# Audio tower on one core: the fused loop over 32 pairs of sequences in another order, relative scores added by TensorE

## What is computed

```python
# t: token mixer
h = depthwise_conv(x, 7 taps) + b_dw; h = relu(w_pw @ h + b_pw); h = max over pairs of rows   # 125 -> 62 rows
y = real(fft2(h)); y = normalised over 192 * gamma + beta
# a: attention with relative positions, 8 heads of 64, values of 96
q = (x @ Wq) * 64**-0.5
scores = (q + r_w_bias) @ k^T + relative_shift((q + r_r_bias) @ r_k^T)
y = softmax(scores) @ v @ Wo + bo
# f: feed-forward with 8-bit activations and ternary weights
xq = clip(round(rmsnorm(x) * 127 / max|.|), -128, 127) / scale
gate, up = split(xq @ w_in^T); y = quantised(rmsnorm(silu(gate) * up)) @ w_out^T
# b: rotary attention, 12 heads of 16 with 3 key heads
# r: router picks one of 8 experts for each row; then the experts, each a gated layer of 512
```

## Time and profile before

| | us |
|---|---|
| median of 3 runs | 1287.79 (1283.11 to 1289.89) |
| the profiled execution | 1298.94 |
| its span, first to last instruction | 1297.1 |
| PE busy | 1066.9 |
| DVE busy | 928.2 |
| ACT busy | 728.9 |
| POOL busy | 350.3 |

### The profile page before, as it was taken

How to read it: one execution, slowest core, us unless ns; L and a number is a source line. 1 busy time by engine, 2 the same in 40 slices (tenths; PEclk the granted TensorE clock), 3 DMA queues, 4 the chain that set the end, 5 groups by cost and what they waited for, 6 DMA issues and landing times.

```text
span 1297.1 us, 30154 instructions
## 1 busy us (share of the span) xinstructions
PE 1066.9 (82%) x9054; PEld 818.0 (63%) x9055; DVE 928.2 (72%) x2959; ACT 728.9 (56%) x2417; POOL 350.3 (27%) x968
## 2 busy tenths in 40 slices
PE   2658998888888888888888888888898652899995
PEld 1536666666666666666666666666666431788884
DVE  2347888888887888888888888888887542355553
ACT  2425766666666666666666666666666430333331
POOL 2012233323322222233332323323322112122222
PEclk9888999999999999999999999999999665899999
DMA  6053011111111111111111111111111004322211
GB/s 202 31 163 91 31 43 35 35 35 37 49 38 42 40 35 35 35 35 35 35 35 35 35 41 35 35 35 36 50 40 35 7 7 157 89 56 58 55 54 40
DMA packets 48910, 65.65 MB, mean 51 GB/s; under 512 B 6573, under 2 KB 39120, under 8 KB 48752
## 3 DMA queue, kind: packets, MB, share of 16 engines
q1 hardware_dynamic: 38656, 46.47, 11.4%
q0 software_dynamic: 4512, 12.52, 2.9%
q10 hardware_dynamic: 5712, 6.29, 1.7%
HBM read 36.61 MB, written 28.95 MB: 51 GB/s over the span
## 4 chain that ended last, share of the span: by engine, by line
issue 49%; DVE 18%; POOL 14%; PE 9%; ACT 5%; DMA 2%; POOLq 1%; SPq 1%; DVEq 0%; ACTq 0%
PE bank_a L566 3%; PE bank_b L566 2%; DVE conv_hi L1137 2%; DVE f_gate L1229 2%; DVE amax_y L1230 1%; POOL rstd_f L513 1%; DVE o L1211 1%; DVE conv_lo L1133 1%; PE bank_t L566 1%; POOL rstd_a L513 1%; POOL rstd_t L486 1%; POOL rstd_b L513 1%; POOL rstd_y L497 1%; POOL hold_a L526 1%; DVE res_b L1271 1%
## 5 line engine op out<-in xcount | busy, mean ns | idle before, releaser
L1133 DVE SCALAR_TENSOR_TENSOR conv_lo<-xT_lo,c_taps,conv_lo 128x248 f32<-128x248 f32 x192 | 90.2, 470 | 25.9 <-ACT conv_hi L900 16.3
L491 POOL TENSOR_TENSOR var_y<-ssq_y,c_eps 128x1 f32<-128x1 f32 x32 | 6.1, 190 | 357.2 <-ACT f_sq L1000 357.2
L978 ACT ACTIVATE b_in<-res_b,norm_shift_f,rstd_f 128x192 f32<-128x192 f32 x32 | 17.5, 546 | 120.0 <-POOL norm_shift_f L516 120.0
L1029 ACT ACTIVATE p<-bank_b,max 128x62 f32<-128x62 f32 x384 | 80.6, 337 | 6.1 <-DVE max L1308 6.1
L566 PE MATMUL bank_a<-e_xT,w_now 128*128 128x128 f32 x544 | 70.5, 284 | 12.1 <-DVE e_gate L1420 9.0
L1299 DVE TENSOR_TENSOR kBD_lo<-bank_b,c_blocks 128x1024 f32<-128x1024 f32 x32 | 39.2, 1224 | 56.3 <-PE bank_b L569 56.3
L566 PE MATMUL bank_a<-c_wv,a_xT 64*64 64x384 f32 (+1 forms) x512 | 78.7, 500 | 0.1
L566 PEld LDWEIGHTS bank_a<-e_xT,w_now 128*128 128x128 f32 x544 | 64.9, 196 | 21.4 <-DVE w_now L1416 11.0
L1415 DVE COPY w_now<-w_sb 128x512 f32 x34 | 14.5, 427 | 86.8 <-PE bank_a L566 78.4
L566 PE MATMUL bank_a<-c_wo,oT 128*128 128x192 f32 x384 | 74.9, 347 | 1.9 <-ACT oT L866 1.9
L566 PE MATMUL bank_a<-a_xT,c_wq 64*128 64x128 f32 (+1 forms) x512 | 74.8, 288 | 1.6 <-ACT a_xT L866 1.6
(11 more groups left out here) (259 smaller groups left out, 3138.9 us busy)
## 6 DMA issues: line engine op xcount, KB each, us to landing
rel_scores<-rel_tok SPq DMA_DIRECT2D x32, 492.0 KB, 2.6
rel_skew<-rel_scores SPq DMA_DIRECT2D x64, 124.0 KB, 2.8
x_tok<-in_x SPq DMA_DIRECT2D x32, 187.5 KB
e_rest<-routed SPq DMA_DIRECT2D x34, 97.0 KB
e_tok<-routed SPq DMA_DIRECT2D x34, 96.0 KB, 1.9
routed<-pad_rows SPq DMA_DIRECT2D x8, 386.0 KB, 2.9
w_sb<-in_w ACTq DMA_DIRECT2D x1, 3072.0 KB, 12.2
...
```

Of the source, the lines that this page charges most:

```text
L978: nc.scalar.activation(dst, src, ACT.Identity, scale=rstd[k][:, :], bias=shift[k][:, :]).then_inc(done, 1)
L1029: last = nc.scalar.activation(p1[:, h, 0:T], src[:, at * T:(at + 1) * T], ACT.Exp, bias=max1[:, h:h + 1])
L1133: c.mark(v.scalar_tensor_tensor(conv_lo[:, :, :], xT_lo[:, :, k:k + PAIRS], c_taps[:, 0, k:k + 1], conv_lo[:, :, :], ALU.mult, ALU.add))
```

## The change

The stages get another order on all engines, and other lags: the whole of part b but its residual now lies in one turn (lag 4), the end of f (`f_transpose_y`, `f_down`) goes from lag 4 to lag 3, the end of a (`a_transpose_heads`) from 3 to 2, its beginning (`a_transpose`) from 2 to 1. POOL's lags are one higher than before, since its list begins at another stage. Beside the order, these stages do other work:

- **Relative scores.** `a_scores` leaves its accumulation open, and a new stage `a_add_relative` on PE multiplies the identity with `rel_skew` (128 rows, 496 columns) onto the same bank. DVE takes only the maxima, from the bank, and ACT the exponentials, from the bank. `s` and L1197 are gone. `rel_tok` and `rel_skew` have the head ahead of the position, so the copy back from DRAM is made of runs of 62 numbers (248 bytes) where it had runs of 248 numbers (992 bytes).
- **The bias of q.** DVE computes `qr` only; ACT makes `qw` from it with four additions of the difference of the biases (`a_bias_qw`).
- **Quantising.** DVE stops at the scale (`scale_of`). ACT rounds in two steps (`f_round_x`, `f_round_y`), POOL multiplies out the `dequant` factors. The clip at 127 falls away.
- **Key blocks.** `kBD_lo` has four blocks instead of eight; `b_scores` multiplies 64 rows at a time, six products of 248 columns where there were two of 496 and two of 248.
- **Token mixer.** The last 64 channels of the two sequences lie at partitions 0 and 64, so that `t_pointwise` has products of 124 columns for each half, `t_pool` and `t_relu` half the elements in their second instruction, and `t_dft` one product on 128 rows and two of 64.

```diff
+            def a_add_relative(m):
+                pe.wait_ge(a_rel, 32 * m + 32)
+                mm(pa1[:, 0:H0 * T].rearrange("p (h a s) -> p h a s", h=HP, a=2), ident[:, :],
+                   rel_skew[:, :, :, :].rearrange("p a h s -> p h a s"), start=False).then_inc(a_s, 1)
...
             def a_max_scores(m):
-                dve.wait_ge(a_s, 2 * m + 2)
-                dve.wait_ge(a_rel, 32 * m + 32)
-                c.link(v.tensor_tensor(s0..., pa1..., rel_skew..., ALU.add))
-                v.tensor_reduce(max0[:, :], s0[:, :, :], axis=AX.X, op=ALU.max, negate=True).then_inc(a_shift, 1)
+                dve.wait_ge(a_s, m + 1)
+                v.tensor_reduce(max0[:, :], pa1[:, 0:H0 * T]..., op=ALU.max, negate=True).then_inc(a_shift, 1)
...
-                    last = nc.scalar.activation(p0[:, h, 0:T], s0[:, h, :], ACT.Exp, bias=max0[:, h:h + 1])
+                    last = nc.scalar.activation(p0[:, h, 0:T], pa1[:, h * T:(h + 1) * T], ACT.Exp, bias=max0[:, h:h + 1])
...
+            def a_bias_qw(m):
+                act.wait_ge(a_qrr, m + 1)
+                after_previous(act, a_s, m)
+                for hp in range(HP):
+                    last = nc.scalar.activation(qw[:, hp, :], qr[:, hp, :], ACT.Identity, bias=bias_step[:, hp:hp + 1])
+                last.then_inc(a_qwr, 1)
...
+                def stage(m):     # f_round
+                    act.wait_ge(qsc_ready[k], m + 1)
+                    nc.scalar.activation(work, work, ACT.Identity, scale=qsc[k][:, 0:1], bias=magic[:, 0:1]).then_inc(rounded_of[k], 1)
+                    act.wait_ge(rounded_of[k], m + 1)
...
+                    nc.scalar.activation(dst, work, ACT.Identity, bias=magic[:, 1:2]).then_inc(done, 1)
...
-                        rel_skew[TP * b:TP * b + TP, :, :, :].rearrange("p a s h -> p a (s h)"),
-                        bass.AP(rel_dram.tensor, b * TP * 2 * RW + (T - 1) * HP,
-                                [[2 * RW - HP, TP], [RW, 2], [1, T * HP]])).then_inc(a_rel, 16)
+                        rel_skew[TP * b:TP * b + TP, :, :, :].rearrange("p a h s -> p (a h) s"),
+                        bass.AP(rel_dram.tensor, b * TP * 2 * RW + T - 1,
+                                [[2 * RW - 1, TP], [REL, 2 * HP], [1, T]])).then_inc(a_rel, 16)
...
             overlapped(pe, (
...
+                (1, t_transpose), (3, a_output), (2, a_project), (4, b_transpose), (4, b_project), (2, a_relative),
+                (1, t_pointwise), (4, b_transpose_qk), (2, a_project_v), (3, f_transpose_x), (4, b_scores),
```

280 lines of the change are left out of this document (149 added, 131 removed).

## The result

| | before | after |
|---|---|---|
| median, us (measured together) | 1288.39 (1283.11 to 1289.89) | 1219.70 (1216.75 to 1221.79) |
| the profiled execution | 1298.94 | 1219.23 |
| its span | 1297.1 | 1217.4 |

The ratio is 0.9462, 95% interval 0.9433 to 0.9491: 68.7 us less. The forecast was 1220.

A forecast was written before the change was run, and what follows sets the result against it. No engine was full: a circle of waits through DVE and PE, plus PE's half clock, set the 30.7 us turn. PE's 25.6 plus waits gave 28.7; 28 turns save 56 us, ends 12: 1220 us, range 1168 to 1274.

The forecast's parts named there:

- The circle and the clock: Old turn: DVE's list is in the circle of waits some 19 us, PE's some 10; half clock costs 1.7 us.
- Rival B: The low clock stays or ACT's rounding is dearer: turn 29.4 to 30.4, 1243 to 1271 us; chance 0.18.
- Work taken from DVE between those points shortens the turn at once: Between the transposed keys from PE and DVE's residual, where DVE works almost without a gap; no separate size given.
- a walk through the new lists: New stage lists followed once round until PE's start came back: turn 28.55 us, taken as 28.7.
- DVE and ACT: Busy time per turn: DVE 4.0 us less, to 21.7; ACT 3.6 more, less 0.3, to 23.8.
- PE at full clock: PE's work per turn: 27.25 - 1.7 + 0.84 - 0.4 - 0.4 = 25.6 us, making it the fullest engine.
- The waits of PE: Six waits in PE's new list, together 2.95 us a turn on top of its work.
- The copy back: `rel_skew` through DRAM lands 6.0 to 7.9 us after `rel_tok`; PE's product comes at 8.5, so the wait is hidden.
- rival E: Short runs cost over 0.09 us, so PE waits for the copy; 1340 or 1414 us; chance 0.08 with ACT as hub.
- The ends: The ten partly filled turns at both ends of the loop save 12 us, between 0 and 20.
- The sum: 28 turns x (30.7 - 28.7) = 56 us, ends 12: 68 us off the median 1287.79, giving 1220.
- the first sign of being right: A piece in the profile's chain of waits that comes back every 28.7 us.

The follow-up runs named there:

- the filler: The kernel before, with two unused products of 256 columns on PE ahead of its wait for `b_in`: 1252.8 us, ratio 0.9689.
- the run with late copies: The kernel after, with three more pairs of copies back issued ahead of the used one: 1308.5 us, ratio 1.0112 to the kernel before.

## Why the prediction was right, and where it wasn't

**The circle and the clock** (its first part) held. The half-clock stretch was put at 1.7 us a turn; the filler gave 1.6 back, and PE's busy time fell by 1.66. The stretch is 3.4 us long by its own row (537.00 to 540.40). Rival B, that it stays in each turn, didn't happen, but the reason against it was only half right: the hole in the second half of the turn does lower the clock behind it, in 4 of the 26 turns of the profiled execution, and that costs 4 to 6 us.

**"Work taken from DVE between those points shortens the turn at once"** was wrong as it stands. In the old order it shortened nothing (1.0164, and 1.003 with y's rounding back on DVE and the clock mended), and the chain of waits there runs through DRAM, in another circle of the same length. I had read the circle of the kernel before and not asked for the next one. The forecast was spared that, since it was made from a walk through the new lists.

**DVE and ACT:** 25.66 - 4.0 = 21.7, measured 21.5; 23.8, measured 24.1. **PE at full clock:** 25.6, measured 25.59. In it the new product was too cheap: 0.84 predicted, 0.94 start to start. The scores of b take 1.05 us from the first start to the last end (539.55 to 540.60). The prediction had 1.25 before and 0.85 after; the rows of before give 1.47 (517.88 to 519.35), so both were read 0.2 too low, and the 0.4 saved, the top of its range, came out all the same.

**The waits of PE** were predicted as 2.95, measured 2.34 plus small gaps. Of the six, four are there: `b_project` (0.6 predicted, 0.52), the probabilities of a (0.9, 0.89), `f_transpose_y` (0.4, 0.31), `f_down` (0.5, 0.46). The two others, for the transposes of b's queries (0.3) and the values of b (0.25), aren't there. The turn is 28.04 where all is at full clock and 28.19 on average, for 28.7.

**The copy back** was the step furthest off. It was to be there 6.0 to 7.9 us after `rel_tok`, and I took 7.9, with 0.6 us to spare. It is there after 6.4: the landing takes 3.1 us for the 2.8 of the earlier trace rows, so 768 more runs cost 0.3 us on the path and not 1.9. The pages' lines of that DMA queue, before and after, give the price of a run (packets, MB, share of 16 engines' span):

```profile
q1 hardware_dynamic: 38656, 46.47, 11.4%
```

```profile
q1 hardware_dynamic: 63232, 46.66, 13.0%
```

The packets grow by 24576, which is 768 for each of the 32 tiles. Their time grows from 11.4% of 16 x 1297.1 us to 13.0% of 16 x 1217.4, by about 170 us: 5 us a tile, or 0.3 us over 16 engines, the same 0.3. In the packet records a run of 248 bytes takes 0.021 us on average and one of 992 bytes 0.061. The 0.04 us a run that the prediction drew from the earlier trace rows, where other traffic lands too, was about twice too dear. The product comes 8.8 us after `rel_tok` (8.5 in the walk), which leaves the 2.4 us that the run with late copies measured as well. That run also showed that rival E's mechanism is real, with its place right: 4.3 us of delay make the kernel 1.1% slower than before.

The Trainium skill, "DMA: Bandwidth & Descriptors", section "Specifications", gives 512 bytes as the least transfer at line rate and says that smaller ones are read, modified and written. The trace after shows 0.021 us for a run of 248 bytes against 0.061 for one four times as long, and those 0.3 us in all, at a DMA share of 0.13 over the turn; it doesn't show how such a run is written.

**The ends** were put at 12 us and gave 8.4 (2.1 and 6.3). **The sum:** 28 turns of 2.0 and 12 for the ends were 68; the profiled pair had 64.3 and 8.4, and 7.0 from the expert loop, which the prediction counts at nothing. Between the medians it is 68.7. The turns gained more than predicted and the ends less, so that the agreement to 1 us is partly luck: the two errors, 8 us and 4, have opposite signs, and the kernel before had a profiled execution 11 us above its median. Of these 11 the expert loop's 7.0 may be the greater part; what the rest is, no run shows. Two slips changed nothing: the range counts rival B with 0.17 and up to 1268, where the list has 0.18 and 1271; and the first sign of being right, a piece every 28.7 us in the chain of waits, can't be looked for, since the chain doesn't reach back to the full turns.

What stays open: why the half clock comes in some turns of the kernel after and not in others with the same wait of 0.89 us; what the new order alone gives with its clock mended; and whether a better place for the product in the old order would make the new work pay there.
